# A two-layer graph network on one core: setup phases merged, x loaded at the start behind the edge lists, three feature blocks computed ahead

## The chip, the cores and the metric

The kernel runs on one core of a Trainium2 chip, as a single launch. The metric is the device time of that launch in microseconds, lower is better. The core has five engines with instruction queues of their own: PE (TensorE, matrix products), DVE (VectorE), ACT (ScalarE), POOL (GpSimd) and SP (SyncE, which here only issues transfers). They meet through semaphores. Transfers issued by SP and by ACT run on the same 16 DMA engines.

## What is computed

```
h = relu(layernorm(x))                       # x: 3750 nodes, 256 features
feat[n, r] = h[n] @ conv_weights[r]          # 8 relations, 4 heads of 64
el, er = attention scores of feat as source, as destination
e = leaky_relu(el[type, src] + er[type, dst]); alpha = softmax of e over the edges of one dst
x = x + segment_sum(alpha * feat[type, src], dst) + h_bias
h = relu(layernorm(x));  h = h @ W_in + b_in
for l in range(3):
    h = relu((mean of h[src] over the edges of each dst) @ W_agg[l] + h @ W_self[l] + b_hid[l])
x = x + h @ W_out + b_out
```

There are 63750 edges, sorted by destination. The edge lists (src, dst, type) are inputs in HBM.

## The kernel before

The kernel is a chain of phases. Each phase is one `nc.Block()`: every engine gets its part of the work in it, and at its end all five engines meet in a barrier, so that no engine begins the next phase before the slowest has run out its queue. The setup phases, in order:

1. First block (lines 327 to 386). SP issues 12 transfers of the edge lists (dst twice, src, type, three pieces each). ACT issues 18 transfers: two attention vectors spread over all 128 partitions (1 MB each, lines 341 to 343) and the convolution weights in 16 pieces of 128 KB (lines 344 to 348). POOL fills constants. DVE waits for the lists (line 383) and converts them to floats.
2. `tile_ends()` and a check block (lines 393 to 452): the first and last key of each column of edges, and flags that say whether the edges are sorted. `sort_edges` and the second `tile_tables` (line 722) run only if a flag says so; for these inputs they are skipped, but their barriers are met.
3. `tile_tables(0, CR)` (lines 613 to 721): DVE, PE, ACT and POOL build index tables; SP stores masks, destinations and pairs of (code, column) to HBM tables.
4. The window phase (lines 740 to 859). DVE runs a chain of small steps (lines 747 to 805), each waiting for the one before, which counts at which edge each of 235 windows of 16 nodes begins; the answer is `edge_i`. PE does counting products for it. POOL builds rows of masks (`csx`, `cbx`, `cnx`, lines 827 to 838), stored by SP in 12 transfers (line 857). SP also loads all of x (lines 844 to 846, 3.7 MB) and the four small vectors.
5. The layernorm phase (lines 889 to 994). DVE and POOL multiply weights by attention vectors and sum them (lines 911 to 919 and 932): the "attention sums". Then DVE, ACT and PE go over eight chunks of 512 nodes: statistics, scaling, transposes into `hT`, score products (`elr`). SP meanwhile runs `load_pairs` (lines 222 to 230) for the first ten blocks of nodes, 78 transfers of 3 KB whose addresses it reads from `edge_i`, and behind them, in the same queue, the eight stores of `er_tab` (line 988).
6. The main block. It begins with the window and feature stage: for each of 30 blocks of 128 nodes, four feature products (`q`, line 1325: 2 products of 512 columns each, on the trace 4 matmul records) evicted and stored by ACT (lines 1181 to 1188), and the 235 windows (3 products each, line 265, made of one-hot tiles that DVE writes, lines 254 and 255, evicted by ACT, line 273) spread over the blocks by `BLOCK_W`, 7 or 8 a block. POOL's gathers of features (line 1141) begin when all 120 feature stores have landed. The attention turns, the second layernorm and the three aggregation layers follow, each fed by the one before.

The few lines on which the reading hangs: the loads, one register each, in `load_pairs`, and the queue order of SP in the layernorm phase.

```
for k, at in enumerate(edge_starts(sp, FIRST_W[b], BLOCK_W[b])):
    sp.dma_start(pairs_in[...], edges[bass.ds(at, DEPTH * P), :]...).then_inc(s_cl[b % 4], 16)
...
for b in range(EARLY):          # SP, layernorm phase; EARLY = 10
    load_pairs(sp, b)
over_chunks(sp, store)
sp.wait_ge(s_et, 16 * NC)
```

Of the kernel before, what the change touches and what calls it, by code (L numbers as in the profile page):

```python
# [34 lines left out]
P = 128  # L35
# [4 lines left out]
NC = 8  # L40
# [26 lines left out]
BLOCK_W = [NREAL * (b + 1) // NBLK - NREAL * b // NBLK for b in range(NBLK)]  # L67
# [32 lines left out]
def gnn_kernel(nc, x, src, dst, etype, conv_w, attn_l, attn_r, h_bias, w_in, b_in, w_agg, w_self,  # L100
               b_hid, w_out, b_out, out):
    ctx = ExitStack()
    with ctx:
        gat = ExitStack()
# [88 lines left out]
        rel = sb("rel", [P, 8, DEPTH])  # L193
        edge_i = sb("edge_i", [1, NTW], I32)
        lo_i = sb("lo_i", [1, NTW], I32)
        past_i = sb("past_i", [1, NTW + 1], I32)

# [41 lines left out]
        def shift_codes(dve, b):  # L239
# [7 lines left out]
            dve.wait_ge(s_rel, b + 1)  # L247
# [61 lines left out]
        s_ld, s_xl, s_at = [nc.alloc_semaphore(a) for a in ("vectors_loaded", "all_x_loaded", "weights_in")]  # L309
        lists_i = stg[:, 5000:5000 + CQ + NTW].bitcast(I32)  # L310
        prod = [stg[:, 4096 + 2048 * i:4096 + 2048 * (i + 1)] for i in range(2)]
# [13 lines left out]
        attn = [side[:, 2048 * i:2048 * (i + 1)] for i in range(2)]  # L325

        with nc.Block() as block:
# [142 lines left out]
        def sort_edges(flag, key_array, other_array):  # L470
# [18 lines left out]
            with nc.Block() as block:  # L489
# [42 lines left out]
                def _(dve):  # L532
                    with when(dve, flag):
                        for v, buf in zip((0, PADSRC, 0), raw_s):
# [77 lines left out]

        def tile_tables(c0, c1, flag=None):
# [11 lines left out]
            with nc.Block() as block:  # L625
                @block.vector
                def _(dve):
                    with when(dve, flag):
# [19 lines left out]
                        for i, to in enumerate((typ_t, dstloc, fidx_i, code_t, col_t)):  # L648
# [6 lines left out]
                            while at < c1 * P:  # L655
# [15 lines left out]
                                at = end  # L671

# [13 lines left out]
                def _(pool):  # L686
                    with when(pool, flag):
# [9 lines left out]
                        c.link(pool.tensor_copy(dst16[:, 0:nc_, :], cut(dstm)))  # L697

# [15 lines left out]
                def _(act):  # L714
                    with when(act, flag):
# [9 lines left out]
        s_w, s_wc, s_ws, s_ri, s_rw, s_xz = (sem("window_steps"), sem("windows_counted"), sem("window_sums"),  # L725
                                             sem("row_masks"), sem("row_masks_stored"), sem("x_zeroed"))
        begun = stg[:, 1792:1792 + CT * NTW].rearrange("p (c w) -> p c w", c=CT)
        PARTS_T = P // GRAIN
        room = hT[:, :, :].rearrange("p k n -> p (k n)")
# [6 lines left out]
        cbx = stg[0:1, 7800:7800 + NS * U].rearrange("p (s t) -> p s t", s=NS)  # L736
        cnx = work[0:1, 8192:8192 + NS * U].rearrange("p (s t) -> p s t", s=NS)
        subs_of = lambda a: a[0:1, 0:NS * U].rearrange("p (s t) -> p s t", s=NS)
        DUP = 14
# [1550 lines left out]
```

## Time and profile before

| | us |
|---|---|
| median of three runs | 2076.78 (2074.4 to 2078.51) |
| the profiled execution, its own time | 2072.4 |
| its span in the trace | 2070.6 |
| first block ends | 19.0 |
| main block's first window product | 157.5 |
| first gather | 533.0 |

The profiled execution is one run, 4.4 us below the median. PE is busy for 86% of the span, DVE for 52%, ACT for 55%, POOL for 25%. In the profile a row of the timeline gives the start, the duration from the start of the first to the end of the last instruction of the row (rows with "xN" group N neighbours), the engine and line, what is written from what, and the idle time before it with its releaser. "ACTq" and "SPq" rows are the issuing of transfers, which takes time of that engine's queue.

### The profile page before, as it was taken

What the parts mean: (1) busy time and instruction counts of PE and PEld (TensorE: products, weight loads), DVE (VectorE), ACT (ScalarE), POOL (GpSimd) and SP (SyncE); (2) the same over time, 40 slices, a digit from 0 to 9 for tenths busy, and PEclk for the clock granted to TensorE, in tenths of its full rate; (3) what the DMA queues carried; (4) which work ended last, traced back from release to release, by engine and by line L of the source; (5) the groups of instructions that cost most, each with busy time, mean ns of one, the idle gap of its engine ahead of it and who ended that gap; (6) DMA issues with size and microseconds to landing.
All of it is one profiled execution on the core that took longest, in us unless ns stands there. A gap on an engine that the chain in (4) does not pass through costs nothing. (4 is left out here: it accounts for less than half of the span.)

```text
span 2070.6 us, 26209 instructions
## 1 busy us (share of the span) xinstructions
PE 1778.8 (86%) x7604; PEld 1236.5 (60%) x7605; DVE 1081.7 (52%) x3126; ACT 1143.4 (55%) x2498; POOL 521.1 (25%) x544
## 2 busy tenths in 40 slices
PE   1159999999497879798797955999989999999998
PEld 1054444444375557565575634777777777877777
DVE  4858888888365676766767535453550000301011
ACT  0034455565387779797787734454545444544442
POOL 2600000000577777777777300000000000000000
PEclk7569999999687789797898887999999999999999
DMA  4314555555655566565665325333324333363432
GB/s 129 82 14 152 171 195 192 181 201 199 202 146 161 152 182 176 153 188 159 171 173 161 101 63 181 99 123 107 110 77 128 113 116 112 98 208 123 135 123 62
DMA packets 285221, 290.67 MB, mean 140 GB/s; under 512 B 88673, under 2 KB 248102, under 8 KB 284806
## 3 DMA queue, kind: packets, MB, share of 16 engines
q1 hardware_dynamic: 235094, 186.23, 29.3%
q0 software_dynamic: 23952, 66.46, 12.1%
q10 hardware_dynamic: 26016, 36.15, 4.8%
q8 instruction: 64, 1.05, 0.2%
q14 instruction: 95, 0.78, 0.1%
HBM read 201.26 MB, written 87.48 MB: 139 GB/s over the span
## 5 line engine op out<-in xcount | busy, mean ns | idle before, releaser
L1141 POOL DMA_INDIRECT work<-feat_tab,fidx_i x499 | 477.6, 957 | 586.0 <-issue 581.2
L2117 PE MATMUL PS<-a_pe,y_hi 128*128 128x512 f32 (+2 forms) x1440 | 556.7, 392 | 33.4 <-ACT a_pe L2014 33.4
L2117 PE MATMUL PS<-a_pe,y_lo 128*128 128x512 f32 (+2 forms) x1440 | 536.7, 379 | 0.0
L2014 ACT ACTIVATE a_pe<-a_in 128x1536 fp32r<-128x1536 f16 (+1 forms) x240 | 329.3, 1376 | 342.7 <-PE PS L2117 329.1
L2117 PEld LDWEIGHTS PS<-a_pe,y_hi 128*128 128x128 f32 (+1 forms) x1440 | 274.0, 190 | 103.1 <-ACT a_pe L2014 35.0
L1210 ACT ACTIVATE work<-work 128x64 f32<-128x64 f32 x1344 | 325.1, 332 | 0.0
L2117 PEld LDWEIGHTS PS<-a_pe,y_lo 128*128 128x128 f32 (+1 forms) x1440 | 274.2, 190 | 55.2 <-issue 6.7
L1385 PE MATMUL PS<-work,stg 128*128 128x260 f32 x1008 | 289.6, 437 | 6.5 <-ACT work L1210 4.6
L1385 PEld LDWEIGHTS PS<-work,stg 128*128 128x128 f32 x1008 | 207.5, 217 | 65.0 <-issue 19.6
L255 DVE TENSOR_SCALAR side<-iota_c,work 128x512 f16<-128x512 f16 x705 | 245.8, 349 | 0.0
L1325 PE MATMUL PS<-wbuf,hT 128*128 128x512 f32 x480 | 226.9, 595 | 0.0
L2221 DVE TENSOR_TENSOR mean<-PS,rdeg 128x1024 f32<-128x1024 f32 (+1 forms) x24 | 27.2, 1135 | 363.3 <-PE PS L2117 363.0
L273 ACT ACTIVATE side<-PS 128x512 f16<-128x512 f32 x235 | 128.7, 595 | 142.0 <-PE PS L265 69.6
L254 DVE TENSOR_SCALAR side<-iota_c,rel 128x128 f16<-128x128 f16 x705 | 176.9, 251 | 49.1 <-PE PS L265 48.3
L265 PE MATMUL PS<-side 128*128 128x512 f16 x705 | 173.6, 381 | 24.6 <-DVE side L255 16.1
L265 PEld LDWEIGHTS PS<-side 128*128 128x128 f16 x705 | 68.3, 98 | 151.2 <-DVE side L255 36.1
L1335 PE MATMUL PS<-er_win,stg 128*128 128x32 f32 x1008 | 134.9, 294 | 22.5 <-ACT stg L1196 22.5
L1335 PEld LDWEIGHTS PS<-er_win,stg 128*128 128x128 f32 x1008 | 129.9, 211 | 26.4 <-ACT stg L1196 24.5
L1325 PEld LDWEIGHTS PS<-wbuf,hT 128*128 128x128 f32 x480 | 91.8, 191 | 75.1 <-issue 57.9
L1181 ACT ACTIVATE stg<-PS 128x512 f32<-128x512 f32 x120 | 72.0, 600 | 43.3 <-PE PS L1325 42.5
L1588 DVE TENSOR_TENSOR work<-work,PS 128x1024 f32<-128x1024 f32 x42 | 51.3, 1221 | 69.1 <-ACT work L1202 69.1
L1579 DVE TENSOR_TENSOR stg<-PS,dstloc 128x512 f32<-128x512 f32 x126 | 86.4, 686 | 1.5
(257 smaller groups left out, 1674.0 us busy)
## 6 DMA issues: line engine op xcount, KB each, us to landing
a_in<-a_tab SPq DMA_DIRECT2D x210, 384.0 KB, 3.2
feat_tab<-stg ACTq DMA_DIRECT2D x120, 260.0 KB, 2.2
a_tab<-side SPq DMA_DIRECT2D x235, 128.0 KB, 1.8
stg<-dst_tab SPq DMA_DIRECT2D x42, 384.0 KB, 4.0
work<-feat_tab,fidx_i POOLq DMA_INDIRECT x499
h_tab<-outs SPq DMA_DIRECT2D x42, 130.0 KB, 2.6
h_tab<-outs SPq DMA_DIRECT2D x8, 520.0 KB, 3.9
stg<-h_tab SPq DMA_DIRECT2D x8, 520.0 KB, 4.1
```

The costliest lines, as they stand in the source:

```text
L254: dve.tensor_scalar(code[:, s, :], iota_c[:, 0:P], rel[:, k, j:j + 1], None, ALU.is_equal)
L255: dve.tensor_scalar(other[:, s, :], iota_c[:, :], pairs_in[:, w, j, 1:2], None, ALU.is_equal).then_inc(built.pair, 1)
L265: pe.matmul(PS[:, BBS[w % len(BBS)], :], code[:, s, :], other[:, s, :], start=(j == 0), stop=(j == DEPTH - 1)).then_inc(built.free, 1)
L273: act.activation(counts[:, w % KEPT_W, :], PS[:, BBS[w % len(BBS)], :], ACT.Copy).then_inc(built.evicted, 1)
L1141: pool.indirect_dma_start(out=ring[:, s, 0:FE], out_offset=None, in_=feat_tab[:, :], in_offset=bass.IndirectOffsetOnAxis(ap=idx, axis=0)). ...
L1210: ins = act.activation(a, a, ACT.Copy, scale=ring[:, s, F + h:F + h + 1])
L1325: mm = pe.matmul(PS[:, cc, :], hT[:, k, b * P:(b + 1) * P], wc[:, k, cc * 512:(cc + 1) * 512], start=(k == 0), stop=(k == K2 - 1))
L1335: mm = pe.matmul(PS[:, ERB, u * RH:(u + 1) * RH], onehotT[:, u * P:(u + 1) * P], er_win[:, :], start=True, stop=True)
L1385: mm = pe.matmul(PS[:, OUTS[j], 0:EXT], onehot[:, t, :], ring[:, j * U + t, 0:EXT], start=(t == 0), stop=(t == U - 1), skip_group_check=True)
L1579: dve.tensor_tensor(onehot[:, q * QT:(q + 1) * QT, :], IOTA_PS.unsqueeze(1).to_broadcast([P, QT, P]), dstloc[:, tiles_of(i, j, q, QT)].uns ...
L2014: act.activation(a_pe[:, load % A_PE, :, 0:n], a_in[:, load % A_IN, :, 0:n], ACT.Copy).then_inc(s_conv, 1)
L2117: mm = pe.matmul(SUMS(ug, n)[:, f, :], y[0:rows_of, kb, f * P:(f + 1) * P], a_pe[0:rows_of, load % A_PE, kb % KB, 0:n], start=(kb == 0 and ...
```

## The change

- `AHEAD = 3`: blocks 0 to 2 get no windows; the 235 windows are spread over blocks 3 to 29, 8 or 9 a block. The first ten blocks with windows now hold 87 of them instead of 78.
- First block: ACT waits for all edge lists before it issues its 18 transfers; SP, when the lists have landed, loads all of x and the four small vectors there. The block has the same barrier at its end.
- The attention sums move into `tile_tables(0, CR)`, behind its other DVE and POOL work.
- The window phase and the layernorm phase become one block. DVE does the layernorm chunks first, then the window chain. SP stores `er_tab` per chunk, then the mask rows, then waits for the end of the window chain (`s_wd`) and only then runs `load_pairs` for ten blocks. PE and ACT do the 12 feature products and stores of blocks 0 to 2 in this block.
- The index rows lie in a buffer of their own instead of in `hT`; x is zero-padded in the first block; the semaphores and buffers move accordingly.

The diff, cut to its core (`keep`, `step` and the pieces that only move are left out):

```diff
-BLOCK_W = [NREAL * (b + 1) // NBLK - NREAL * b // NBLK for b in range(NBLK)]
+AHEAD = 3
+BLOCK_W = [0] * AHEAD + [NREAL * (b + 1) // (NBLK - AHEAD) - NREAL * b // (NBLK - AHEAD) for b in range(NBLK - AHEAD)]
...
-            dve.wait_ge(s_rel, b + 1)
+            dve.wait_ge(s_rel, b - AHEAD + 1)
...
+        def sum_features(pe, q):
+            b, cc = divmod(q, 4)
+            if q >= 4:
+                pe.wait_ge(s_fe, 2 * (q - 3))
+            for k in range(K2):
+                mm = pe.matmul(PS[:, cc, :], hT[:, k, b * P:(b + 1) * P], wc[:, k, cc * 512:(cc + 1) * 512],
+                               start=(k == 0), stop=(k == K2 - 1))
+            mm.then_inc(s_fm, 1)
+
+        def keep_features(act, q):
+            b, cc, slot = q // 4, q % 4, q % 2
+            act.wait_ge(s_fm, q + 1)
+            if q >= 2:
+                act.wait_ge(s_fs[slot], 16 * (q // 2))
+            act.activation(fout[:, slot, :, 0:F], PS[:, cc, :].rearrange("p (r f) -> p r f", r=2), ACT.Copy
+                           ).then_inc(s_fe, 1)
+            act.copy(fout[:, slot, :, F:FE],
+                     elr[:, b, 0, 2 * cc * H:(2 * cc + 2) * H].rearrange("p (r h) -> p r h", r=2)
+                     ).then_inc(s_fe, 1)
+            act.wait_ge(s_fe, 2 * q + 2)
+            act.dma_start(feat_tab[0:PADSRC * R, :].rearrange("(n r) f -> n r f", r=R)[
+                b * P:(b + 1) * P, 2 * cc:2 * cc + 2, :], fout[:, slot, :, :]).then_inc(s_fs[slot], 16)
...
-        s_ld, s_xl, s_at = [nc.alloc_semaphore(a) for a in ("vectors_loaded", "all_x_loaded", "weights_in")]
+        s_ld, s_xl, s_at, s_xz, s_xr = [nc.alloc_semaphore(a) for a in (
+            "vectors_loaded", "all_x_loaded", "weights_in", "x_zeroed", "x_ready")]
+        (s_fm, s_fe, s_et) = [nc.alloc_semaphore(a) for a in ("feat_summed", "feat_kept", "el_stored")]
...
+        index_rows = early.enter_context(nc.sbuf_tensor("index_rows", [P, 9 * T], FP32))
...
-            return hT[:, :, :].rearrange("p k n -> p (k n)")[:, i * T:(i + 1) * T].rearrange(
-                "p (c j) -> p c j", c=CT)
+            return index_rows[:, i * T:(i + 1) * T].rearrange("p (c j) -> p c j", c=CT)
...
+        def load_all_x(sp, turn=1):
+            sp.wait_ge(s_xz, turn)
+            sp.dma_start(x_all[:, 0:FULL, :], x[0:FULL * P, :].rearrange("(b p) f -> p b f", p=P)).then_inc(s_xl, 16)
+            sp.dma_start(x_all[0:N - FULL * P, FULL, :], x[FULL * P:N, :]).then_inc(s_xl, 16)
 
...
+                sp.wait_ge(s_rl, 48 * 4)
+                load_all_x(sp)
+                for buf, v in ((hb_b, h_bias), (bout_b, b_out)):
+                    sp.dma_start(buf[:, :], v.rearrange("(o n) -> o n", o=1).to_broadcast([P, F])).then_inc(s_ld, 16)
+                sp.dma_start(bin_c[:, :], b_in.rearrange("(k p) -> p k", p=P),
+                             allow_slow_non_contiguous=True).then_inc(s_ld, 16)
+                sp.dma_start(bh_c[:, :, :], b_hid.rearrange("l (k p) -> p l k", p=P),
+                             allow_slow_non_contiguous=True).then_inc(s_ld, 16)
...
+                act.wait_ge(s_rl, 48 * 4)
...
+                dve.memset(x_all[:, FULL:32, :], 0.0).then_inc(s_xz, 1)
...
+        def attention_sums(dve):
+            dve.wait_ge(s_at, 16 * (K2 * R + 2))
+            for i in range(2):
+                dve.tensor_tensor(prod[0], wc[:, 0, :], attn[i], ALU.mult).then_inc(s_pr, 1)
+                dve.wait_ge(s_pr, 3 * i + 1)
+                for k in range(K2):
+                    if k == 1:
+                        dve.wait_ge(s_pp, i + 1)
+                    dve.tensor_reduce(wlr[:, k, i * RH:(i + 1) * RH], prod[k].rearrange("p (c d) -> p c d", d=D), AX.X,
+                                      ALU.add).then_inc(s_pr, 1)
+                    dve.wait_ge(s_pr, 3 * i + k + 2)
+
+        def attention_products(pool):
+            pool.wait_ge(s_at, 16 * (K2 * R + 2))
+            for i in range(2):
+                if i == 1:
+                    pool.wait_ge(s_pr, 3)
+                pool.tensor_tensor(prod[1], wc[:, 1, :], attn[i], ALU.mult).then_inc(s_pp, 1)
 
...
+                    if flag is None:
+                        attention_sums(dve)
...
+                    if flag is None:
+                        attention_products(pool)
...
-                dve.memset(x_all[:, NBLK - 1:32, :], 0.0).then_inc(s_xz, 1)
...
+                with when(dve, 0):
+                    dve.memset(x_all[:, FULL:32, :], 0.0).then_inc(s_xz, 1)
+                dve.wait_ge(s_xr, 1)
+                ln_stats(dve, x_rows(0), 0, 0, s_bs, s_vr)
+                over_chunks(dve, step)
+                keep(NC - 2, 0)
+                keep(NC - 1, 1)
+
...
+                dve.sem_inc(s_wd, 1)
...
-            @block.sync
-            def _(sp):
-                sp.wait_ge(s_xz, 1)
-                full = NBLK - 1
-                sp.dma_start(x_all[:, 0:full, :],
-                             x[0:full * P, :].rearrange("(b p) f -> p b f", p=P)).then_inc(s_xl, 16)
...
+                act.wait_ge(s_ee, NC)
+                for q in range(4 * AHEAD):
+                    keep_features(act, q)
...
+                pe.wait_ge(s_ht, 2 * NC)
+                for cc in range(4):
+                    sum_features(pe, cc)
+                pe.wait_ge(s_ee, NC)
+                for g in range(PARTS_T):
+                    pe.wait_ge(s_w, g + 2)
...
+                for q in range(4, 4 * AHEAD):
+                    sum_features(pe, q)
...
+                sp.wait_ge(s_xl, 32)
+                with when(sp, 0):
+                    load_all_x(sp, 2)
+                    sp.wait_ge(s_xl, 64)
...
-                for b in range(EARLY):
+                over_chunks(sp, store)
+                sp.wait_ge(s_ri, 12)
+                at = 0
+                for a, n in ((csx, U + 1), (cbx, U), (cnx, U)):
+                    for h in range(H):
+                        sp.dma_start(rm_tab[:, at:at + n].unsqueeze(0), a).then_inc(s_rw, 16)
+                        at += n
+                sp.wait_ge(s_rw, 16 * 3 * H)
+                sp.wait_ge(s_wd, 1)
+                for b in range(AHEAD, AHEAD + EARLY):
                     load_pairs(sp, b)
-                over_chunks(sp, store)
                 sp.wait_ge(s_et, 16 * NC)
 
         end_phase()
...
-                for b in range(NBLK):
+                for b in range(AHEAD, NBLK):
```

## Rows read from the trace of the kernel before

**Rows 1.** The page: span, and the group of feature products.
```profile
span 2070.6 us, 26209 instructions
...
L1325 PE MATMUL PS<-wbuf,hT 128*128 128x512 f32 x480 | 226.9, 595 | 0.0
```
**Rows 2.** Busy time of each engine over the window and feature stage.
```profile
157.00:531.00 374.00, 362.46 (x1185) 160.01 (x1185) 316.71 (x1441) 203.88 (x475) 0.00 (x0) 0.99 0.56 186
```
**Rows 3.** Timeline of PE inside that stage: start, duration, engine, line, count.
```profile
301.59 1.46 PE L265 MATMUL PS<-side 128*128 128x512 f16 x6
302.88 1.88 PE L1325 MATMUL PS<-wbuf,hT 128*128 128x512 f32 x4
304.60 0.59 PE L265 MATMUL PS<-side 128*128 128x512 f16 x2
```
**Rows 4.** Timeline of the main block's first window product.
```profile
157.46 1.01 PE L265 MATMUL PS<-side 128*128 128x512 f16 x2 [16.14 <-DVE side L255]
```
**Rows 5.** SP's transfers of ten blocks' pairs; er_tab, with its landing (last line).
```profile
84.76 3.56 SPq L228 DMA_DIRECT2D work<-pair_tab  x7
...
84.76 58.85 SPq L228 DMA_DIRECT2D work<-pair_tab  x78
143.66 5.61 SPq L988 DMA_DIRECT2D er_tab<-stg  x8
...
DMA to landing us min/median/max: 1.8/1.8/1.9
```
**Rows 6.** Timeline of the first block: ACT's and SP's issues, DVE.
```profile
1.64 16.92 ACTq L346 DMA_DIRECT2D wbuf<-in_L_gnn_conv_weights  x16
...
1.45 0.46 SPq L332 DMA_DIRECT2D hT<-in_dst  x1
...
2.92 0.45 SPq L332 DMA_DIRECT2D hT<-in_dst  x1
...
15.70 1.43 DVE L385 CAST hT<-hT 128x512 f32<-128x512 int32 x4 [12.14 <-DMA hT<-in_edge_type]
19.02 0.17 DVE L400 COPY small<-hT 128x7 f32<-128x7 f32 x1 [1.89 <-PEq L327]
```
**Rows 7.** DMA queues from 8 to 9 us (q1 is SP's, q10 is ACT's).
```profile
q1 hardware_dynamic: 408, 0.20, 68.4%
q10 hardware_dynamic: 421, 0.10, 47.3%
```
**Rows 8.** The queue of ACT, 3 to 6.5 us (attention vectors), then 16 to 20 us (weights).
```profile
q10 hardware_dynamic: 167, 1.24, 94.1%
...
q10 hardware_dynamic: 3680, 0.92, 112.8%
```
**Rows 9.** The queue of SP, 56 to 65 us, while it loads x.
```profile
q1 hardware_dynamic: 3096, 3.17, 107.7%
```
**Rows 10.** Timeline of DVE: last step of the tables, first of the window phase.
```profile
49.34 0.69 DVE L652 COPY col_t<-PS 128x512 f32<-128x512 f32 x1
52.10 0.70 DVE L743 MEMSET work<- 128x768 f32 x1 [2.08 <-PEq L625]
```
**Rows 11.** Timeline of DVE in the window chain: a tiny step, and the last.
```profile
62.00 1.39 DVE L751 TENSOR_SCALAR small<-hT 128x7 f32<-128x7 f32 x1
...
79.83 0.14 DVE L805 COPY cuts_i<-turns_i 1x1 int32<-1x1 int32 x1
```
**Rows 12.** Timeline of DVE in the attention sums.
```profile
83.23 6.63 DVE L914 TENSOR_TENSOR stg<-wbuf,side 128x2048 f32<-128x2048 f32 x1 [3.25 <-PEq L740]
89.89 4.61 DVE L918 TENSOR_REDUCE wlr<-stg 128x32 f32<-128x2048 f32 x2
94.53 2.29 DVE L914 TENSOR_TENSOR stg<-wbuf,side 128x2048 f32<-128x2048 f32 x1
```
**Rows 13.** Timeline of DVE: first and last step of the eight layernorm chunks.
```profile
103.62 0.75 DVE L870 BATCH_NORM_STATS2 stats<-work 128x6 f32<-128x256 f32 x2
...
141.35 0.42 DVE L897 TENSOR_SCALAR stg<-PS 128x256 f32<-128x256 f32 x1 [1.36 <-PE PS L961]
```

More of the change, by code:

```diff
@@ L739, in gnn_kernel, with ln_stats, ln_finish @@
         DUP = 14
+        hN = side[:, 0:2048].rearrange("p (s b f) -> p s b f", s=2, b=4)
+        hTs = side[:, 2048:4096].rearrange("p (s k n) -> p s k n", s=2, k=K2)
+        def ln_stats(dve, rows, c, slot, stats_done, var_ready):
+            for b in range(4):
+                dve.bn_stats(stats[:, slot, b, :], rows(b)).then_inc(stats_done, 1)
+            dve.wait_ge(stats_done, c * 4 + 4)
+            dve.sem_inc(passed, 1)
+            for b in range(4):
+                dve.bn_aggr(mv[:, slot, b, :], stats[:, slot, b, :]).then_inc(var_ready, 1)
+        def ln_finish(dve, rows, c, slot, std_done, rstd_done, hn_ready, to):
+            dve.wait_ge(std_done, c + 1)
+            dve.reciprocal(rstd[:, slot, :], std[:, slot, :]).then_inc(rstd_done, 1)
+            dve.wait_ge(rstd_done, c + 1)
+            for b in range(4):
+                dve.tensor_scalar(to[:, b, :], rows(b), mv[:, slot, b, 0:1], rstd[:, slot, b:b + 1],
+                                  ALU.subtract, ALU.mult).then_inc(hn_ready, 1)
+        s_bs, s_vr, s_sd, s_rs, s_hn, s_tp, s_ht, s_el, s_ee = [sem(x) for x in (
+            "stats_done", "var_ready", "std_done", "rstd_done", "hn_ready", "hn_turned", "ht_ready",
+            "el_ready", "el_kept")]
         with nc.Block() as block:
@@ L805, in _ @@
                 c.link(dve.tensor_copy(cuts_i[0:1, NC:NC + 1], turns_i[0:1, 0:1]))
-            @block.tensor
-            def _(pe):
-                for g in range(PARTS_T):
-                    pe.wait_ge(s_w, g + 2)
-                    for c in range(CT):
-                        pe.matmul(PS[0:1, 7, 0:NTW], one_c, ended[:, g, c, :], start=(g == 0 and c == 0),
-                                  stop=(g == PARTS_T - 1 and c == CT - 1))
-                for c in range(CT):
-                    pe.matmul(PS[0:1, 5, 0:NTW], one_c, ended[:, PARTS_T - 1, c, :], start=(c == 0), stop=(c == CT - 1))
-                pe.wait_ge(s_w, PARTS_T + 3)
-                for c in range(CT):
-                    mm = pe.matmul(PS[0:1, 6, 0:NTW], ones[:, 0:1], begun[:, c, :], start=(c == 0),
-                                   stop=(c == CT - 1))
-                mm.then_inc(s_wc, 1)
+                dve.sem_inc(s_wd, 1)
             @block.gpsimd
@@ L979, in _ @@
                 halves(NC - 1, (NC - 1) % 2)
+                pe.wait_ge(s_ht, 2 * NC)
[4 more added lines that the diff above has]
+                    pe.wait_ge(s_w, g + 2)
+                    for c in range(CT):
+                        pe.matmul(PS[0:1, 7, 0:NTW], one_c, ended[:, g, c, :], start=(g == 0 and c == 0),
+                                  stop=(g == PARTS_T - 1 and c == CT - 1))
+                for c in range(CT):
+                    pe.matmul(PS[0:1, 5, 0:NTW], one_c, ended[:, PARTS_T - 1, c, :], start=(c == 0), stop=(c == CT - 1))
+                pe.wait_ge(s_w, PARTS_T + 3)
+                for c in range(CT):
+                    mm = pe.matmul(PS[0:1, 6, 0:NTW], ones[:, 0:1], begun[:, c, :], start=(c == 0),
+                                   stop=(c == CT - 1))
+                mm.then_inc(s_wc, 1)
+                for q in range(4, 4 * AHEAD):
+                    sum_features(pe, q)
             @block.sync
@@ L1315, in _ @@
                 w = 0
-                for b in range(NBLK):
+                for b in range(AHEAD, NBLK):
                     for cc in range(4):
-                        q = 4 * b + cc
                         for _ in range(BLOCK_W[b] // 4 + (cc < BLOCK_W[b] % 4)):
@@ L1484, in _ @@
                 w = 0
-                for b in range(NBLK):
+                for b in range(AHEAD, NBLK):
                     many = BLOCK_W[b]
@@ L1670, in _ @@
                 w = 0
-                for b in range(NBLK):
+                for b in range(AHEAD, NBLK):
                     if b + EARLY < NBLK:
```

146 lines of the change are left out of this document (38 added, 108 removed).

## The prediction

> **What bounds the kernel now.** I read the page first: PE is the busiest engine of the span [rows 1], but the change touches only the time before the first gather, so the question is what ends last in each stretch there. In the window and feature stage PE is busy 362 of 374 us at a granted clock of 0.99 [rows 2]. Inside it, six window products begin 1.29 us before the next feature product, 0.215 each, and four feature records take 302.88 to 304.60, so one `q` costs 1.717 us and one window 0.646 [rows 3]. 120 x 1.717 + 235 x 0.646 = 358 us: the stage, from 157.46 on [rows 4], is PE's, with some 13 us of stalls. Whatever delays its begin delays the end one for one, since the gathers and all that follows are fed from it.
>
> Before it, the setup is a chain of barriers, each reached last by another engine. First block: ACT, which issues until 1.64 + 16.92 = 18.56, while DVE is done at 17.13; DVE goes on at 19.02 [rows 6]. Tables: DVE's last step ends at 50.03, the window phase starts at 52.10 [rows 10]. Window chain: DVE, until 79.97 [rows 11]. Layernorm phase: DVE from 83.23 [rows 12] to 141.77 [rows 13], but what ends the phase is SP: 78 pair loads from 84.76 to 143.61, then eight er_tab stores to 149.27 and 1.8 us of landing [rows 5]. So the pair loads, 59 us, run beside 58.5 us of DVE work and cost about nothing; only the stores behind them stick out, by 9 us.
>
> **First block after.** With the lists alone, 12 issues at the spacing of the first four, (2.92 - 1.45) / 3 = 0.49 us, end at 7.3; with the landing of 1.8 us [rows 5] they are in at 9.1 instead of 15.7 [rows 6]. But DVE doesn't go on when the lists are in: the barrier waits for ACT, and ACT now begins its 18 issues at 9.1 instead of 0.74. Before they took 17.8 us beside the lists (1 MB). Now they run beside x (3.84 MB). The queues' speeds: attention vectors 1.24 MB in 3.5 us, 0.35 MB/us, weights 3680 packets in 4 us, 920/us alone [rows 8], x 3096 in 9 us, 344/us alone [rows 9]. Where both queues had work they moved packet for packet, 408 and 421 [rows 7]. So: first bytes at 10.4, vectors 2.1 MB with 256 packets of x between them 6.6 us, to 17.0; a pair of one weight and one x packet 1/920 + 1/344 = 4.0 ns, 3490 pairs 14.0 us, to 31.0; the remaining 4700 weight packets 5.1 us and some 2 us for the small vectors, to 38. ACT's last issue ends about one landing time, 1.8 us [rows 5], before its data are in, at 36.3, and DVE goes on at **36.8 instead of 19.0: +17.8**. Bounds: if x took nothing from ACT's queue, 9.1 + 17.8 + 0.5 = 27.4 (+8.4); if the queues wait for all of both, 38.5 (+19.5). I take the packet-for-packet value, since rows 7 show that rule at work on these two queues.
>
> The Trainium skill (DMA: Bandwidth & Descriptors, Queues, rings and completion order) says that a DMA engine turns between queues by packets of some 9 to 17 descriptors, 4096 B preferred; by bytes a weight queue with 256 B descriptors would then get four of them for each of x. This case's rows have the counts equal, not the bytes; by the page's reading ACT would end some 2 us earlier, an estimate.
>
> **Tables and attention sums.** The work from 19.02 to 50.03 is the same, 31.0 us, to 67.8. POOL's first product now runs beside DVE's last table steps; the first attention product took 6.63 us beside POOL and 2.29 with POOL behind it [rows 12], so up to 4.3 us can be lost; the table steps that it meets read PSUM mostly, I take 1.5. Then the sums without that clash: 2.29 + 4.61 = 6.9, and from 94.53 to 103.6 [rows 12, 13] 9.1 more: 16.0 instead of the 20.4 from 83.23. To 85.3. The barriers behind the tables (50.03 to 52.10, rows 10) 2.1, and the new branch on the flag before DVE may read x, which no row shows (0 to 3; between a barrier and SP's first load, which also reads a register, lie 1.5 us, rows 12 and 5), 2.0: to 89.4. x and the vectors have landed at 38, so they cost nothing more here.
>
> **Merged block.** Layernorm chunks 103.62 to 141.77, 38.2 us [rows 13]. POOL's mask rows, until now beside the window chain, now run beside the first chunks. What that does to DVE shows in a 7-element step of 1.39 us [rows 11]; such waits are 1.2 us each, nine or so of them would be 11: 0 to 12, I take 5. To 132.6. Window chain: 52.10 + 0.70 to 79.97, 27.2 us [rows 10, 11], less the same waits, 3.5 (0 to 5): to 156.3. The er_tab stores go per chunk and are hidden; the mask rows, 12 issues at 5.61 / 8 = 0.70 us [rows 5], are 8.4 us behind the last of them, hidden under the window chain's 23.7.
>
> The Trainium skill (SBUF — State Buffer, section on the shared port) has DVE's two-port and two-input operations and a POOL operation that reads SBUF exclude each other for a whole instruction. By it the layernorm could wait nearer to the 12 than to the 5; that makes the time worse by 7, an estimate.
>
> **Pair loads.** They now stand on SP behind `s_wd`, the end of DVE's last work of the block. Behind them on SP is only the end of the block, but all five engines wait for that barrier. One load costs 3.56 / 7, 0.51 us; 78 are 40.1 of the 58.85, so each of the nine passages to the next block's addresses costs 2.08 [rows 5]. 87 loads: 44.7 + 18.7 = 63.4, and 1.5 from the start to the first load: **64.9 us with nothing beside them** but 12 feature products on PE and ACT (each 1.7 to 3.4 us of PE and a store, some 30 us: hidden). To 221.2. From the end of the last issue and landing before, 151.1, to the first window product 157.46 is 6.4 [rows 4, 5]: first product at **227.6 instead of 157.46: +70.1.**
>
> **Window stage.** 12 of 120 `q` are gone: 12 x 1.717 = **-20.6 us**. The windows are the same 235. 8.7 a block instead of 7.8 put more DVE and ACT work beside each `q`; stalls were 13 us, they may shrink by a tenth or grow: -2 to +10, I take 0. Ends of this term: -24 to -11. Between gathers and end nothing is changed.
>
> **Sum.** 17.8 + 1.5 (tables) - 4.4 (sums) + 2.0 (branch) + 5 (layernorm) - 3.5 (chain) - 4.0 (the gap 79.97 to 83.23 and the memset, gone) and then, since the phase ended at 151.1, 9.3 us behind DVE's last step, and now 64.9 behind it, + 55.6: 70.0, as above but for rounding. Less 20.6: +49.5. 2072.4 + 49.5 = 2121.9 for the profiled execution; the median lies 4.4 above that one before: **2126**.
>
> **Rivals.** (a) ACT's queue gets its way and the first block ends at 27.4: -9.4, 2117. For it: the attention vectors held the lists back until 7 us; against: rows 7. (b) Each feature block taken out saves its whole share of the stage, (531 - 157.46) / 30 = 12.5, not 6.9, because the windows fit under something else: -16.6, 2109. Against it: PE is busy through [rows 2]. (c) The wait does more harm: stage stalls grow by 10 with uneven 9 windows a block: 2136. (d) The lists don't come earlier alone, for instance because their issues are slow by themselves (in at 15): +6, 2132. (e) The other side: the main block doesn't wait for SP's whole queue. If the other engines went on when the chain is done and only the first block's loads (8, some 5.6 us) had to be in, 64.9 would be 5.6, and the time 2067. It decides from the point where less than 64.9 - 49.5 = 15.4 us of the loads is exposed. Against it: before, no engine had anything from 141.8 to the end of SP's stores and the first product came behind them [rows 4, 5, 13]; and the semaphores are cleared behind that barrier.
>
> **How the numbers follow.** Forecast 0.50, (a) 0.15, (b) 0.08, (c) 0.10, (d) 0.07, (e) 0.04; 0.06 for what I haven't named, a third of it around no change. The likeliest is 2126. The bounds of the single terms, -9.4 and +1.7 for the first block, -6.5 and +13 for the contention, -3.4 and +10 for the stage, -4 and +3 for loads and branch, don't come together; with (a), (c), (d) and half of (b) inside, the range is 2102 to 2146. What a measurement of this kernel can tell from no change is about 0.2%, 4 us. Faster needs (e): 0.04; same 0.02; slower 0.94.
>
> **What would show each step.** Right: ACT's 16 weight issues ending near 36 and DVE's first copy of the next block behind them; the lists converted near 9; 87 pair loads in one run of about 63 us with DVE idle; first window product near 228; the stage some 20 us shorter, still PE's. Wrong: the first block ending below 28; loads overlapping DVE work; a stage shorter than 345 us; the first gather less than 40 us later than 533.

## The result

The change made the kernel slower: 2135.9 us median of four runs (2132.3 to 2137.4) against 2075.6 (2073.3 to 2078.5) beside it on the same chip, a ratio of 1.029 (95% interval 1.027 to 1.031). The profiled execution took 2135.95 us, 63.5 more than the one of before. The forecast for it was +49.5; the 14 us between the two come from one term, the window stage.

The page of the changed kernel, its span and the group of its feature products, answers [rows 1]; the second fence is the busy time of each engine over its window and feature stage, in two parts (columns as in [rows 2]):

```profile
span 2133.7 us, 26192 instructions
...
L289 PE MATMUL PS<-wbuf,hT 128*128 128x512 f32 x480 | 227.3, 600 | 0.0
```
```profile
224.00:470.00 246.00, 226.07 (x733) 97.03 (x734) 204.29 (x935) 122.02 (x285) 0.00 (x0) 0.97 0.51 166
470.00:591.00 121.00, 121.00 (x405) 53.23 (x404) 109.49 (x505) 72.72 (x164) 0.00 (x0) 1.00 0.60 206
```

In the first part PE is idle for 20 of 246 us, in the second for nothing. The last pair load is issued at 461, so the idle time is in the stretch with pair loads. The same split of the kernel before, where the last pair load is issued at 405, leaves 8.7 us idle in the first part:

```profile
157.00:405.00 248.00, 239.29 (x778) 105.24 (x779) 209.82 (x955) 130.53 (x308) 0.00 (x0) 0.99 0.54 177
405.00:527.00 122.00, 121.83 (x406) 54.49 (x405) 106.33 (x485) 72.05 (x164) 0.00 (x0) 1.00 0.59 205
```

The setup of the changed kernel, from its timeline (start, duration, engine, line, count, and in brackets the idle time before and what ended it), answers [rows 4 to 6, 10, 11 and 13]:

```profile
8.99 1.43 DVE L432 CAST index_rows<-index_rows 128x512 f32<-128x512 int32 x4 [3.96 <-DMA index_rows<-in_edge_type]
9.35 12.93 SPq L362 DMA_DIRECT2D work<-in_x  x1
10.11 25.70 ACTq L392 DMA_DIRECT2D wbuf<-in_L_gnn_conv_weights  x16
36.27 0.17 DVE L447 COPY small<-index_rows 128x7 f32<-128x7 f32 x1 [25.85 <-PEq L364]
...
61.51 4.60 DVE L705 TENSOR_SCALAR index_rows<-index_rows 128x512 f32<-128x512 f32 x1
...
156.58 8.60 SPq L231 DMA_DIRECT2D work<-pair_tab  x14
...
221.81 0.71 DVE L1499 MEMSET outs<- 128x780 f32 x1 [66.79 <-PEq L134]
...
224.78 2.72 PE L268 MATMUL PS<-side 128*128 128x512 f16 x6 [65.50 <-DVE side L258]
```

The lists are in at 8.99, and that gains nothing: DVE converts them and then stands 25.85 us, until 36.27, behind a barrier that ACT reaches last (its last weight is issued at 35.81). Later it stands 66.79 us, from 155.02, the end of the window chain, to 221.81, behind a barrier that SP reaches last (the last of 87 pair loads is issued at 218.10). These two lines are most of the price of the change. Boundary by boundary, in us from the start of the span:

| | before | forecast | after |
|---|---|---|---|
| first block ends | 19.0 | 36.8 | 36.3 |
| tables end | 50.0 | 69.3 (67.8 + 1.5) | 71.4 |
| layernorm | 103.6 to 141.8 | 89.4 to 132.6 | 90.4 to 132.3 |
| window chain ends | 80.0 | 156.3 | 155.0 |
| first window product | 157.5 | 227.6 | 224.8 |
| stage, first to last PE product | 370.3 | 349.7 | 366.3 |
| of it PE stalled | 12.7 | 12.7 | 29.3 |

Here and below "stalled" is the sum, over PE's products of the stage, of the time to the next one beyond 0.216 us (window) or 0.429 us (feature record), the spacings of an unbroken run. So the first window product was forecast within 3 us, too late, and the stage 16.6 us too short. From the end of the stage to the end of the kernel the two take the same time: the first to the last gather 631.7 us in both.

### The profile page after: what moved, and what is told of

It reads as the page before. It is cut to its first block and busy times, and to the rows that moved or that the text cites. A ratio compares the mean times of both kernels' runs of the same rounds, so it can differ in the third digit from the quotient of the medians.

```text
span 2133.7 us, 26192 instructions
## 1 busy us (share of the span) xinstructions
PE 1779.1 (83%) x7604; PEld 1232.1 (58%) x7605; DVE 1078.8 (51%) x3123; ACT 1143.2 (54%) x2498; POOL 514.8 (24%) x544
## 5 line engine op out<-in xcount | busy, mean ns | idle before, releaser
L2043 ACT ACTIVATE a_pe<-a_in 128x1536 fp32r<-128x1536 f16 (+1 forms) x240 | 329.3, 1376 | 342.5 <-PE PS L2146 329.1
L2250 DVE TENSOR_TENSOR mean<-PS,rdeg 128x1024 f32<-128x1024 f32 (+1 forms) x24 | 27.2, 1135 | 363.2 <-PE PS L2146 363.0
L2130 PE MATMUL PS<-wbuf,hT 128*128 128x256 f32 x360 | 85.3, 391 | 1.9 <-ACT hT L2054 1.9
```

The lines of the kernel that those rows point to most:

```text
L2043: act.activation(a_pe[:, load % A_PE, :, 0:n], a_in[:, load % A_IN, :, 0:n], ACT.Copy).then_inc(s_conv, 1)
L2130: mm = pe.matmul(PS[:, 6 + b // 2, (b % 2) * F:(b % 2 + 1) * F], hT[:, k, u * CQ + b * P:u * CQ + (b + 1) * P], weight[:, k, :], start=(k ...
```

## Experiments

Four edits (ACT without its wait, the chain first, no blocks ahead, loads between the stores) ran on a chip on which the kernel before took 2262.3 us (2255.4 to 2266.0). The stretch from first to last gather takes 815 to 820 us there instead of some 632. What comes ahead of it keeps the times of the first chip where the program is the same: the setup within 1 us (first window product 224.62 and 224.78), the window stage within some 3 us (366.3 to 369.6). The changed kernel as it is was not run on that chip. So ratios compare with the kernel before on the same chip, and the mechanism is read from the boundaries ahead of the first gather. The other edits ran on two chips on which the kernel before took 2074.6 and 2073.9 us. All edits are to the changed kernel unless the text says otherwise; they are shown cut to their core, "..." marks what is left out.

**ACT doesn't wait for the lists.** SP's order stays: lists, then x.

```diff
-                act.wait_ge(s_rl, 48 * 4)
```

> The changed kernel, but ACT issues the attention vectors and weights at once, as in the kernel before; x stays behind the lists on SP. Theory (the first block's end is the last issue of ACT, held back 8.2 us by the wait and slowed by x): the lists are in near 15.5 again, nearly all weights are issued by then, and the block ends with SP, which issues x (0.4 and some 6.5 us for the second piece, which waits for room) and the four vectors (2.6 us): near 25.5 instead of 36.3, the whole 10 to 11 us shorter, 2125. Rival (the block's end goes by the bytes in flight, 7.9 MB in all, whoever is first): the block ends at 30 to 33, the whole 4 to 6 us shorter, 2131.

Timeline of this kernel:

```profile
1.65 21.12 ACTq L391 DMA_DIRECT2D wbuf<-in_L_gnn_conv_weights  x16
...
15.99 7.97 SPq L362 DMA_DIRECT2D work<-in_x  x1
...
27.51 0.88 SPq L381 DMA_DIRECT2D bh_c<-in_L_gnn_b_hid  x1
28.84 0.17 DVE L446 COPY small<-index_rows 128x7 f32<-128x7 f32 x1 [11.77 <-PEq L364]
```

The block ended at 28.84: 7.4 earlier than in the changed kernel, and the first window product came 7.5 earlier, at 217.27. ACT is done at 22.77; now SP ends the block, since a transfer of x holds its issuer for 7.97 us and four small vectors stand behind it. The theory named SP as the new last one and was 3 us too low on how long it takes (28.8 is between its 25.5 and the rival's 30 to 33, but the rows show SP issuing to the end, as the theory had it). So even without the wait the block is 10 us longer than before, because x's issues are inside it. Ratio 1.027 (1.024 to 1.030).

**x only in the merged block.** The lists alone, ACT behind them, and x with its vectors issued at the merged block's start.

The four small vectors move with x.

```diff
-                sp.wait_ge(s_rl, 48 * 4)
-                load_all_x(sp)
...
-                sp.wait_ge(s_ld, 16 * 4)
-                sp.wait_ge(s_xl, 32)
...
+                load_all_x(sp)
```

> The changed kernel, but x and the four vectors are loaded at the begin of the merged block, as the kernel before did in its window phase; ACT still waits for the lists. Theory (the first block's end is ACT's last issue, slowed packet for packet by x): with x away the vectors need 5.8 us and the weights 8.9 at the speed they had alone, from 10.4 on: the last issue ends near 23.2 and the block at 23.7 instead of 36.3. Of these 12.6 us the layernorm gives back some 11 to 14, since it now waits for x: first window product between 222 and 227. Rival (the wait alone is the cost, x costs nothing beside the weights): the block ends at 35 to 36 as before.

The block ended at 22.84, forecast 23.7. ACT's weights begin at the same time as in the changed kernel and are out 13 us sooner: that is what x does to them on the other queue, the term "packet for packet" of the prediction. The layernorm then waited for x instead, which gave most of it back:

```profile
22.84 0.17 DVE L438 COPY small<-index_rows 128x7 f32<-128x7 f32 x1 [12.29 <-PEq L364]
...
90.61 1.41 DVE L808 BATCH_NORM_STATS2 stats<-work 128x6 f32<-128x256 f32 x4 [13.85 <-DMA work<-in_x]
```

The first window product came at 221.41, 3.4 earlier than in the changed kernel's first trace and 4.7 earlier than in its trace on the same chip (below). Its one run took 2143.2 us, 6 more than the changed kernel's median there, so the total shows no gain.

**The window chain ahead of the layernorm.** DVE's and PE's layernorm code behind the chain, `er_tab`'s stores behind the pair loads.

```diff
-                ln_stats(dve, x_rows(0), 0, 0, s_bs, s_vr)
-                over_chunks(dve, step)
...
                 dve.sem_inc(s_wd, 1)
+                ln_stats(dve, x_rows(0), 0, 0, s_bs, s_vr)
+                over_chunks(dve, step)
...
-                over_chunks(sp, store)
...
+                over_chunks(sp, store)
```

> The changed kernel, but in the merged block DVE and PE do the window chain first and the layernorm behind it, and SP issues the mask rows, the pair loads and then er_tab, so that the pair loads run beside the layernorm as in the kernel before. Theory (87 pair loads of 64 us on SP behind the last DVE step are the cost): the chain ends near 116, the mask rows are stored near 119.5, the loads end near 184, er_tab lands near 191, the first window product comes at 197 to 199 instead of 224.8: 26 to 28 us shorter, 2109. Rival (the loads only hide other work, the layernorm with the features ahead would end as late): first product later than 210, less than 15 us shorter.

```profile
117.81 1.41 DVE L818 BATCH_NORM_STATS2 stats<-work 128x6 f32<-128x256 f32 x4 [1.03 <-issue]
...
120.16 4.21 SPq L231 DMA_DIRECT2D work<-pair_tab  x8
...
149.37 34.29 SPq L231 DMA_DIRECT2D work<-pair_tab  x46
...
183.72 5.63 SPq L1027 DMA_DIRECT2D er_tab<-elr  x8
```

The same pair loads now run from 120.16 to 183.66 beside the layernorm (117.81 to 158.05). First window product at 197.42 instead of 224.78 (224.62 on the same chip in the kernel with the loads between the stores, whose setup is the changed kernel's), -27.4; ratio 1.015 (1.013 to 1.017), where the kernel without ACT's wait and the one without blocks ahead, which keep the changed kernel's order, stand at 1.027 and 1.026 on this chip. The pair loads behind the last DVE work are thus shown as the largest part of the loss. What is left of it is again SP: 25.6 us of loads stick out behind the layernorm, which is why fewer blocks of pairs ahead are tried below.

**No feature blocks ahead.** `AHEAD = 0`; ten blocks of pairs ahead stay.

```diff
-AHEAD = 3
+AHEAD = 0
...
-                for cc in range(4):
-                    sum_features(pe, cc)
```

> The changed kernel with AHEAD = 0: no features ahead, 235 windows over 30 blocks, 7 or 8 a block, 78 pair loads in the merged block. Theory (the features taken out of the stage save 20.6 us of PE and give back 16.6 in stalls, since each block's 9 pair loads hold SP longer before the stores of its windows): first product 4.7 to 6 us earlier (9 loads fewer), stage 370 us with 12 to 13 us of stalls, instead of 366 with 29: the whole within 4 us of the changed kernel, 2135. Rival (features ahead are worth their 20.6 us and the stalls have another cause, which stays): the whole 12 to 16 us longer, 2150.

First window product 3.5 us earlier (221.27; 78 loads instead of 87), a stage of 372.6 us, stalled 15.1. With 12 more feature products than in the changed kernel the stage is only 6.3 us longer instead of 20.6: so it is the blocks ahead that bring most of the added stalls, and not the merged block or x.

**Pair loads between the window stores.** SP issues the loads of the block ten further on one by one, each behind the store of a window, and not in a burst ahead of the block's stores.

```diff
-                        load_pairs(sp, b + EARLY)
-                    for _ in range(BLOCK_W[b]):
-                        window_sp(sp, w)
+            for k in range(max(len(windows), len(starts))):
+                if k < len(windows):
+                    window_sp(sp, windows[k])
+                if k < len(starts):
+                    sp.dma_start(pairs_in[:, FIRST_W[b] + k, :, :].rearrange("p t a -> p (t a)"),
...
```

> The changed kernel, but in the window stage SP issues each block's pair loads one by one between the stores of that block's windows, instead of all ahead of them. Theory (the stall is SP's burst of 8 or 9 loads, some 7 us, in which ACT finds no free slot among 4 because no window store is issued): stalls of PE in the stage fall from 29 us to under 10, the stage from 366 to 345 to 350, the whole 16 to 21 us shorter, 2117. Rival (the stalls come from three windows between two feature products, more than the 4 banks and 8 one-hot slots hold): the stage stays at 360 to 368, the whole within 5 us of 2136.

The stage fell to 341.0 us with 4.0 stalled. Total of what ACT waited for the slots that `a_tab`'s stores free, over the stage (us in total, times, longest), in the changed kernel, in this one and in the kernel before, in this order:

```profile
ACT side L276 <- DMA a_tab<-side: 75.9, 17, 8.1
```
```profile
ACT side L290 <- DMA a_tab<-side: 6.1, 7, 2.1
```
```profile
ACT side L273 <- DMA a_tab<-side: 58.8, 18, 6.1
```

And one such wait in the changed kernel's timeline:

```profile
299.32 4.87 SPq L231 DMA_DIRECT2D work<-pair_tab  x9
...
304.24 4.98 SPq L282 DMA_DIRECT2D a_tab<-side  x7
306.15 0.60 ACT L276 ACTIVATE side<-PS 128x512 f16<-128x512 f32 x1 [7.72 <-DMA a_tab<-side]
...
306.80 0.82 PE L268 MATMUL PS<-side 128*128 128x512 f16 x3 [3.78 <-ACT side L276]
```

A burst of nine loads keeps SP from 299.32 to 304.19. Ahead of it SP reads the nine addresses from `edge_i` into registers: the trace has this one instruction (line 218) from 295.11 for 3.83 us, so SP was held for 9.1 us in all. The window stores stand behind it, their four SBUF slots fill, ACT can't evict the next window until a store has landed at 306.15, and PE stops for 3.78 us because its PSUM banks are full. Ratio 1.017 (1.014 to 1.019).

The reading of addresses is as much a part of the hold as the loads are, and it is what varies: 0.8 to 3.8 us per block in this trace. Counted from its start to the next store, SP is held 7.4 us on average in the changed kernel (17 times) and 6.6 in the kernel before (20 times). The two longest holds of the changed kernel, 9.1 and 9.5 us, are followed by 4.0 and 6.1 us of PE's stalls up to the next hold (one of 7.0 us by 4.3); the six holds under 5.6 us, five of them in the kernel before, by none.

**The same one edit in the kernel before**, and the changed kernel once more on a chip near the first one's speed (before: 2074.6).

> The kernel before with the one change that SP issues each block's pair loads one by one between the stores of the block's windows. Theory (SP's burst of loads makes the stage's stalls): stalls 12.7 us fall to 2 to 5, the stage from 370 to 361, the whole 8 to 10 us shorter, ratio 0.996. Rival (with 8 loads a block the burst fits under the 4 slots, stalls have other causes): unchanged within 3 us.

> The changed kernel unaltered, on the chip of the runs beside it, as their common measure. Both theories: first window product near 224.8, last feature product near 591, the ratio to the kernel before near 1.029.

The changed kernel again: 2137.0, ratio 1.031 (1.027 to 1.035), first window product at 226.13 and a stage of 367.8 us with 30.9 stalled, so such boundaries repeat within some 2 us, from one chip to another too. The kernel before with the edit: first window product where it was (158.04), stage 360.7 instead of 370.3, stalled 3.1 instead of 12.7. Median of ten runs 2059.9, ratio 0.994 (0.992 to 0.997). So 9.6 of the "some 13 us of stalls" that the prediction took as given in the kernel before came from this burst too.

**POOL's product waits for the tables.** One wait ahead of POOL's attention products.

```diff
+                        pool.wait_ge(s_te, 6)
```

> The changed kernel, but POOL's first attention product waits until DVE has done the six small steps of the tables that read SBUF; what is left there reads PSUM. Theory (one DVE step with SBUF input, or two, waits for POOL's whole product, 4.6 us in the changed kernel and again in the version put together): the tables end 31.0 us behind the first block's end instead of 35.2, and the sums still take 16.1: first window product 4 us earlier, 220.6. Rival (POOL's product slows whatever DVE does, PSUM reads too): the tables end 34 to 35 us behind the first block.

DVE in this kernel, where the changed one shows 4.60 for the same step:

```profile
61.14 0.43 DVE L705 TENSOR_SCALAR index_rows<-index_rows 128x512 f32<-128x512 f32 x1
```

Tables in 31.0 us (35.9 to 66.89) as before, and the first window product 4.05 us earlier, at 220.73. The sums took 16.7 instead of 16.0, so holding POOL back costs 0.7 of the 4.2 that it gives; its one execution can't tell 4 us in the total (2133.3). POOL's product now runs from 63.22 for 4.50 us beside steps of DVE that read PSUM, and these keep their times (0.69 us for the last four full-tile copies, before and after): the rival of this edit falls.

**Put together.** ACT issues at once, x is loaded in the merged block, the chain goes first, loads between stores; then the number of blocks ahead is varied. The first version, with six blocks of pairs ahead and POOL waiting for an earlier point (`s_f` at 9):

> A version put together from the findings: ACT at once, x loaded in the merged block, window chain before layernorm, EARLY = 6 (46 pair loads in the merged block, so that they end with the layernorm), no features ahead, loads between the window stores, POOL's first attention product held until DVE's table steps on SBUF are done. Theory (SP's queue and the chain of DVE are what costs): first block 19.0, tables 50, sums 66, chain 95, layernorm 137, first window product 144 to 149, stage 361 to 363, last feature product 507 to 511 instead of 527.8: 17 to 21 us below the kernel before, ratio 0.991. Rival (the merged order costs elsewhere, by contention of DVE with POOL or later loads): within 5 us of the kernel before.

```profile
45.24 4.50 POOL L681 TENSOR_TENSOR stg<-wbuf,side 128x2048 f32<-128x2048 f32 x1 [1.15 <-issue]
```
```profile
45.40 4.39 DVE L713 TENSOR_SCALAR nodeid<-nodebase,iota_p 128x74 f32<-128x74 f32 x1
```

First window product at 152.83, some 4 us later than the top of what was expected: the wait only moved the clash to another step, one of 74 elements, which took 4.39 us beside POOL's 4.50 and takes 0.26 without. Median 2063.1, ratio 0.994 (0.992 to 0.997).

With the wait behind DVE's steps on SBUF, as above (`s_te` at 6), and five blocks of pairs ahead:

> The version put together before, with EARLY = 5 (38 to 39 pair loads, so that er_tab's stores are out when the layernorm ends) and POOL's product behind DVE's SBUF steps; no features ahead. Theory: tables end at 50.4 instead of 54.6, chain near 96, layernorm near 133.5, first window product at 142 to 144 instead of 152.8, last feature product at 502 to 505: 23 to 25 us below the kernel before, ratio 0.988 to 0.989. Rival: something else than SP comes late in the merged block: first window product later than 148.

```profile
45.33 0.26 DVE L713 TENSOR_SCALAR nodeid<-nodebase,iota_p 128x74 f32<-128x74 f32 x1
...
97.05 1.41 DVE L822 BATCH_NORM_STATS2 stats<-work 128x6 f32<-128x256 f32 x4
101.07 7.02 SPq L231 DMA_DIRECT2D work<-pair_tab  x10
...
129.21 6.65 SPq L1030 DMA_DIRECT2D er_tab<-elr  x8
```

39 pair loads are over at 129.16 and the eight stores at 135.86, just behind the layernorm (97.05 to 135.43). First window product at 143.91, stage 360.6, last feature product at 504.53. Median 2049.5 (2047.8 to 2051.2), **ratio 0.988 (0.986 to 0.991)**: 1.2% shorter than the kernel before on the same chip.

The same with three feature blocks (and so nine blocks of pairs) ahead:

> The same with three feature blocks ahead and EARLY = 9 (78 pair loads beside layernorm and features). Theory (features ahead only pay if they lie under something else; here SP's 78 loads of 58 us and er_tab end at 165, later than the features): first window product at 170 to 173, stage 341 to 342 with 4 us of stalls, last feature product at 512 to 514, 10 us later than without features ahead, ratio 0.993. Rival (features ahead are hidden and save their 20.6 us): last feature product below 500, ratio 0.985.

PE and SP behind its layernorm, which ends at 135.48:

```profile
134.85 20.82 PE L303 MATMUL PS<-wbuf,hT 128*128 128x512 f32 x48
```
```profile
100.87 56.22 SPq L231 DMA_DIRECT2D work<-pair_tab  x78
157.15 5.79 SPq L1032 DMA_DIRECT2D er_tab<-elr  x8
```

The 12 feature products ahead are 48 records with nothing beside them on PE: 20.8 us, as much as they cost in the stage. Pair loads and stores end 7 us later still. First window product at 171.06, stage 342.5 (5.5 stalled), last feature product at 513.52, 9.0 later than with none ahead; median 2059.9, ratio 0.993 (0.990 to 0.995). Three feature blocks with only five blocks of pairs ahead wasn't tried; by these lines the phase would then end with PE, 7 us sooner, and the two versions be about even.

And the kernel before with only the loads between the stores and six blocks of pairs ahead instead of ten:

> The kernel before with two changes: pair loads between the window stores in the stage, and EARLY = 6, so that 46 to 47 pair loads instead of 78 stand ahead of er_tab on SP in the layernorm phase. Theory (er_tab's stores stick out 9.3 us behind DVE's last step, since the pair loads end only then): pair loads end near 121, the last er_tab store is issued at 142.5 and lands at 144.3 instead of 151.1; first window product at 150.7 instead of 157.5, stage 360 to 362, together 15 to 17 us below the kernel before, ratio 0.9925. Rival (the loads moved into the stage cost there what they save here): ratio 0.995 to 0.997, as with the interleaving alone.

47 loads end at 119.24, well inside its layernorm, and only the stores stick out; first product at 152.84, stage 360.6. Median 2051.6 (2046.6 to 2060.9, five runs), ratio 0.989 (0.987 to 0.992). Against 2049.5 for the version with everything, the medians don't tell the two apart, although the first gather comes 8.8 us earlier in the latter. So, as far as the medians tell, two small edits of the kernel before gain as much as the version put together, without the merged block. In the profiled executions the whole differs by 11.3 us (spans 2059.1 and 2047.8), but this kernel's profiled run was its slowest of five.

## Why the prediction was right, and where it failed

**First block, +17.8 forecast, +17.3 measured.** The lists came at 8.99 (9.1), ACT's last weight was issued at 35.81 (36.3). The packet-for-packet count of [rows 7] held: while x and the weights run side by side in the changed kernel, their two queues move 249 and 244 packets from 20 to 21 us, 243 and 245 from 24 to 25, 243 and 248 from 28 to 29; and without x the block ended near its forecast (22.84 against 23.7). Rival (a), that ACT's queue gets its way, falls by the 35.81, and (d), that the lists don't come earlier, by the 8.99. The estimate made from the Trainium skill (DMA: Bandwidth & Descriptors, Queues, rings and completion order) puts ACT's last issue 2 us earlier than the sum, 34.3, and is 1.5 us off the trace; the count of packets is 0.5 off.

**Tables, +1.5 forecast, +4.2 measured.** The reason given, that the steps beside POOL's product "read PSUM mostly", missed one that doesn't. It lasted 4.60 us instead of 0.43, as long as POOL's product of 4.82 us that began 0.50 before it. Holding POOL back gave the 4.2 us back, less 0.7 in the sums. The Trainium skill (SBUF — State Buffer, section on the shared port) says that the two engines' conflict blocks the loser for a whole instruction; here the traces agree, in two kernels (4.60 and 4.39), and both steps are short again when POOL waits. On the layernorm the forecast's 5 us was measured as 3.7 (41.9 against 38.2), and the page's reading of 12 did not come: the mask operations there touch one partition, and how they take turns with DVE was not tried by itself.

**Attention sums 16.0, measured 16.0. Barrier and branch, 4.1 forecast, 2.9 measured** between the sums and the layernorm. **Window chain 23.7, measured 22.8.**

**Pair loads, 64.9 forecast, 63.1 measured** (155.0 to 218.1), exposed from end to end. Rival (e), that the main block wouldn't wait for SP's whole queue, falls by the line with 66.79 us of idle DVE, and the chain put first shows the other side of the same account: 27.4 us back as soon as the loads have something beside them.

**Stage, -20.6 forecast, -4.0 measured. This is the step that failed:** "they may shrink by a tenth or grow: -2 to +10, I take 0". The 12 feature products went (the stage's products need 20.6 us less), but stalls rose by 16.6, outside even my upper end; rival (c) named it with 10. What I had not asked is what the 13 us of stalls were. They were counted and carried over as if they belonged to the stage. They belong to the time for which SP is held by a block's addresses and loads, and the change makes that time longer and what covers it shorter. The loads are 8.7 in 4.6 us instead of 7.8 in 4.0, and with the reading of the addresses SP is held 7.36 us on average instead of 6.57. The stage's products take 337.6 us instead of 358.2, so a window comes every 337.6 / 235 = 1.44 us instead of 1.52, and four slots cover 5.75 instead of 6.10 us. An estimate from these: 17 x (7.36 - 5.75) = 27 us of stalls in the changed kernel (29.3 measured) and 20 x (6.57 - 6.10) = 9 in the kernel before (12.7). It is rough: it leaves out the four PSUM banks, which cover more, and the landing of a store (304.24 to 306.15 above), which takes cover away. What is shown and not estimated: stalls go to 4.0 us in the changed kernel and to 3.1 in the kernel before when the loads stand between the stores, and to 15.1 with no blocks ahead. With the loads between, the reading of addresses is still there (2.1 us on average, 3.4 at most), and it doesn't bring the stalls by itself. The cause could have been read from the kernel before: [rows 5] have the price of a load, and the waits of ACT for `a_tab`'s stores, 58.8 us in total, were the second largest of all waits of that stage:

```profile
ACT side L273 <- PE PS L265: 69.6, 78, 19.1
ACT side L273 <- DMA a_tab<-side: 58.8, 18, 6.1
```

A rival inside this, that three windows in a row between features overflow PSUM by themselves, falls too: with loads between stores the pattern of windows is the same and nearly all of the stall is gone. So does the reason that rival (c) gives, the uneven nine windows a block, as a cause by itself: the blocks keep their nine windows with the loads between the stores, and 4.0 us of stalls are left.

Rival (b), that each feature block ahead saves 12.5 us, is the opposite of what came: three of them shortened the stage by 4.0 us. A feature block ahead takes as long ahead as in the stage, and pays only where it lies under other work: in the changed kernel beside DVE's window chain (PE's 48 records run from 131.66 to 159.28, the chain from 132.3 to 155.0); with the chain put first, three blocks ahead (and four more of pairs) shorten the stage by 18.1 us and delay it by 27.2.

**What the sum hid:** setup 2.8 us too late, stage 16.6 too short, together 13.8 too little. The likeliest median, 2126, missed by only 10, since the 4.4 us added for the distance of the median from the profiled execution weren't there in the changed kernel (2135.9 and 2135.95). That the range held the result is owed to the large terms, first block and pair loads, which were right in mechanism and size. That rival (c) has 2136 to the microsecond is luck: its 10 us on the stage were 16.6, and the setup's error and those 4.4 us made up the rest.

## What to carry to other kernels

Waiting for one transfer to be in before issuing the next helps only if the engine that ends the block is the one that waits for that transfer; ask who arrives last at the barrier, and what else has to be issued ahead of it. Transfers that a queue has to issue in any case (here some 0.5 us each, and 0.6 to 3.8 us per set of addresses) want an engine's work beside them, so the step that makes their addresses goes first, and prefetching no deeper than that cover is worth more than prefetching deep. Stalls of a bound engine are a term with a cause: before carrying them over, find what stands on the queue ahead of the transfers that free its buffers, reading of addresses included, and spread it between them.

## What the hardware showed that I had not expected

- The issue of one transfer can hold its engine for long, and longer beside another busy queue: the second piece of x, 38 KB behind one of 3.7 MB, held SP for 6.44 us in the kernel before, with no transfer of ACT beside it, 7.97 in the kernel without ACT's wait, while ACT issued the last of its weights, and 12.93 in the changed kernel, beside all of them. The engine that issues is part of the account, not only the bytes.
- One instruction that reads 7 or 8 addresses from SBUF into registers took SP between 0.55 and 3.7 us in the window stage of the kernel before. No run here tells what sets it, and the timeline's rows don't list it: it shows as a gap between two rows of SP.
- A 74-element DVE step took 4.39 us instead of 0.26 because a POOL product on full tiles had begun 0.16 us before it.
- On one chip the same gathers' stretch took 815 to 820 us instead of some 632, with the setup within 1 us and the window stage within some 3. No run here tells why.
- The order of transfers within one queue alone was worth 9.6 us of the stage in the kernel before (ratio of the whole 0.994), with no transfer more or less.
